# A conv mixer on one core, without three TensorE products per image whose result nothing reads

## The reference: what is computed

```python
h = _layernorm(x, n1_g, n1_b)
p = h @ w_in + b_in                                   # 96 -> 192 channels
local = conv(p, k_conv, 3x3, SAME, one filter per channel)
mixed = 0.25 * (lr + rl + tb + bt) + local            # four decaying scans over the image
mixed = _layernorm(mixed, on_g, on_b)
x = x + (mixed @ w_out + b_out)                       # 192 -> 96 channels
```

## Time and profile before

| | us |
|---|---|
| median of 3 runs | 1312.41 |
| lowest and highest | 1305.92, 1313.32 |
| profiled execution | 1309.46 |
| its span | 1307.7 |
| mixer, first transpose to the last residual | 247.5 to 405.8 |

### The profile page before, as it was taken

The page is one execution under the profiler, slowest core; times in us unless marked ns, Lnnn a source line. Parts: engine busy times, 40 slices in busy tenths (PEclk is TensorE's granted clock), DMA queues, the critical chain, the costliest instruction groups (busy, mean ns, idle before and its releaser), DMA issues. The chain is left out here.

```text
span 1307.7 us, 23695 instructions
## 1 busy us (share of the span) xinstructions
PE 1154.8 (88%) x8859; PEld 790.6 (60%) x8859; DVE 740.0 (57%) x2112; ACT 515.9 (39%) x839; POOL 387.1 (30%) x584
## 2 busy tenths in 40 slices
PE   4888879789887979999999997788888978999998
PEld 2565656566665656766666674466455544577776
DVE  3788844477772436666666666276455565333322
ACT  1555533343431333333343332345343422455543
POOL 3645445443425421010101210424100000353522
PEclk8999969899997989999999998699799999999999
DMA  4500000000000000000000000000000000000000
GB/s 88 100 11 2 2 2 0 1 1 1 2 1 1 0 1 1 1 1 1 1 1 1 1 2 1 1 1 1 1 2 1 2 2 1 2 13 7 9 11 13
DMA packets 28924, 9.39 MB, mean 7 GB/s; under 512 B 26961, under 2 KB 28816, under 8 KB 28816
## 3 DMA queue, kind: packets, MB, share of 16 engines
q1 hardware_dynamic: 25760, 7.02, 2.6%
q10 hardware_dynamic: 3056, 0.92, 0.3%
HBM read 6.36 MB, written 1.57 MB: 6 GB/s over the span
## 5 line engine op out<-in xcount | busy, mean ns | idle before, releaser
L156 POOL TENSOR_TENSOR ln_v<-MV,eps 128x2 f32<-128x2 f32 (+3 forms) x81 | 16.2, 201 | 427.2 <-PE bank L1132 247.3
L1194 ACT ACTIVATE fa_e<-bank 128x1024 f32<-128x1024 f32 x64 | 65.5, 1024 | 161.1 <-PE bank L1102 161.1
L1997 PEld LDWEIGHTS bank<-e_w,ex_G 128*128 128x128 f32 x768 | 90.6, 192 | 14.4 <-issue 14.1
L2112 DVE SCALAR_TENSOR_TENSOR X<-bank,ex_L,X 128x96 f32<-128x96 f32 x128 | 31.8, 311 | 114.0 <-PE bank L1997 108.1
L1246 DVE TENSOR_REDUCE fa_z<-bank 128x4 f32<-128x1024 f32 x64 | 78.3, 1223 | 26.3 <-PE bank L1084 24.7
L1989 PE MATMUL bank<-hT,e_w 96*128 96x512 f32 x192 | 90.6, 609 | 0.0
L1997 PE MATMUL bank<-e_w,ex_G 128*128 128x96 f32 x768 | 90.0, 274 | 0.0
L2040 ACT ACTIVATE ex_G<-bank,e_b 128x512 f32<-128x512 f32 x96 | 64.3, 686 | 61.7 <-PE bank L1989 58.9
L1844 DVE TENSOR_REDUCE ca_z<-bank 128x2 f32<-128x256 f32 x96 | 48.9, 552 | 49.3 <-PE bank L1571 49.2
L1102 PE MATMUL bank<-fa_a,fa_b 64*128 64x256 f32 x512 | 74.1, 409 | 1.1 <-DVE fa_a L1253 1.1
L1115 PE MATMUL bank<-fa_e,fa_v 128*64 128x256 f32 x512 | 72.0, 404 | 1.1 <-ACT fa_e L1194 1.1
(11 more groups left out here) (252 smaller groups left out, 2641.7 us busy)
## 6 DMA issues: line engine op xcount, KB each, us to landing
out_tokens<-X SPq DMA_DIRECT2D x8, 192.0 KB, 2.1
X<-in_x SPq DMA_DIRECT2D x56, 24.0 KB
e_w<-in_L_ffn_w SPq DMA_DIRECT2D x2, 576.0 KB
bias0r<-in_L_conv_rpb_table ACTq DMA_DIRECT2D x16, 24.0 KB
m0w<-in_L_conv_mlp_w SPq DMA_DIRECT2D x2, 144.0 KB
m1w<-in_L_conv_w SPq DMA_DIRECT2D x2, 144.0 KB
f_w<-in_L_ffn_W SPq DMA_DIRECT2D x2, 142.5 KB
mixer<-in_mixer SPq DMA_DIRECT2D x1, 256.0 KB
```

What stands on the lines that cost most here:

```text
L1194: act.activation(E[v % 2][:], k.banks[:, b:b + 2, :].rearrange("p i (c q) -> p i c q", c=2), ACT.Exp).then_inc(s["exp"], 1)
L1997: last = pe.matmul(bank[4 + e % 2][:, t * C:(t + 1) * C], G[e % 2][:, j, t * P:(t + 1) * P], k.ew2[:, e, j, :], start=(j == 0), stop=(j == ...
```

## The change

Three calls of `keep_warm` are deleted. Nothing else is different: every wait, every other product, every buffer and their order stay, on all engines. The loop has 18 steps, and `back` and `conv_t` are each called 16 times, so 50 instructions go.

```diff
                 def back(n):
-                    keep_warm(pe, k, bank[4][:])
                     pe.wait_ge(s["z2"], n + 1)
                     after(pe, s["zTe"], n)
...
                 def conv_t(n, slot):

-                    keep_warm(pe, k, bank[4][:])
                     pe.wait_ge(s["conv"], 9 * (n + 1))
                     pe.wait_ge(s["acc1"], n + 1)
...
                 for n in range(IMAGES + 2):
                     slot = n % 2
-                    keep_warm(pe, k, bank[4][:])
                     if n + 1 < IMAGES:
                         tokens(n + 1, 1 - slot)
```

## The result

The median of 12 runs is 1316.15 us, against 1310.71 us for 12 runs of the kernel before. The medians are 5.4 us apart. The ratio on record is 1.0053, with a 95% interval of 1.0029 to 1.0078; it is that of the means, which are 7 us apart. The change made the kernel slower by 5 to 7 us of 1311, which is within 1% and clear of no change. The profiled execution took 1312.8 us, with a span of 1311.0 us where the one of before had 1307.7.

The account below looks back on a forecast made before the run. TensorE was the busiest mixer engine, with its path and ScalarE's `cm_zT` ending level before `out`. From 1309.5 us, minus 0.3 gain, plus 12.8 for clock falls, gave 1322.0; a third of 2.95 made it 1323, range 1307 to 1336.

Parts of the forecast that it names:

- The product ahead of the wait for `cm_z` costs nothing: Mixer, unread product before TensorE waits for VectorE's norm: removing it gains 0, as the wait ends at the same time.
- The other two gain nothing because `cm_zT` ends level with TensorE's path: Products ahead of `conv_t` and `tokens`: TensorE's path shortens 0.43 us an image, but ScalarE's copy limits gain to 0.3 us together.
- The rival of a gain of 6 us: Mixer: clock holds and `out` starts 0.43 us earlier in each image, giving 1303.5 us; chance 0.04.
- The price of a cold stretch: Taken from window attention: each stretch at low clock costs 1.60 us, with two stretches counted to a fall in the mixer.
- the 10.5 or more that were named as a sign: Between two mixer residuals, an image with a cold stretch was to take 10.5 us or more, against 8.97 to 8.99.
- Eight cold stretches: Mixer: idle gaps make the clock fall in one image in four, 4 falls of two stretches, 12.8 us of loss.
- the 4 to 8 stretches that were to support it: Mixer's granted clock: 4 to 8 stretches at 0.50, beginning near the transposes of `cm_z`, were to support the forecast.
- A fall in nearly each image: Rival for the mixer: longer gaps around the transposes make the clock fall almost every image, 24 us, 1333 us; chance 0.21.
- what was said of them there: A skill page on PE-mode transposes: they do not count as engine activity as products do, giving more falls weight; no size.
- The clock holds: Rival for the mixer: the waits are too short for the clock to fall, 1309 us, no change; chance 0.20.
- The third of 2.95 us that was added for the median of before: Whole kernel: the median of runs lay 2.95 us above the profiled execution; a third of this was added, giving 1323 us.

Follow-up runs that it names:

- the gate was opened: Against the changed kernel: one residual product of `out` ahead of its wait for `cm_zT`, which is signalled in halves, old order kept; 1304.33 us.
- the open form: Against the changed kernel: `out`'s residual products ahead of its wait, `cm_zT` signalled in halves, sums in two PSUM banks, no unread products; 1292.62 us, ratio 0.9877.
- The second profile: The kernel without the unread products executed once more under the profiler, nothing else changed; 1311.59 us.
- the kernel with both sums in one bank: Against the changed kernel: `out`'s residual products ahead of its wait, `cm_zT` signalled in halves, both sums opened in one PSUM bank; 1291.89 us, ratio 0.9881.

## Why the prediction was right, and where it was off

The forecast was 1323 us, with a range of 1307 to 1336. The measured 1316.15 lies in it and is slower than before, within 1%. The mechanism was right, an unchanged path and a few falls of the clock, and the term for the falls was more than twice too large; it is a wide range that covers it.

- *The product ahead of the wait for `cm_z` costs nothing.* Right: the idle time there went from 0.92 to 1.14 or 1.15 us, as predicted. The kernel with three products in this gap shows the same from the other side.
- *The other two gain nothing because `cm_zT` ends level with TensorE's path.* Right: images stayed at 8.98 to 8.99 us, `out` waits 0.32 us in each, and the gain came out once the gate was opened (8.40 us) and went when the products were put back into the open form (8.07 to 8.50). The rival of a gain of 6 us fell for the reason that was given against it.
- *The price of a cold stretch, 1.60 us, two to a fall.* Two to a fall was right. The price was a little high: the first fall made two images 2.7 us longer together, 1.3 us a stretch, and they took 10.2 and 10.4 us by their residuals, not the 10.5 or more that were named as a sign.
- *Eight cold stretches.* This term was mis-sized. It rested on four falls, one image in four, and the profile has two falls, of two stretches each, which is the lower end of the 4 to 8 stretches that were to support it. Two falls at 2.7 us are 5.3 us in place of 12.8. With the 1 us that was added for the median this gives 1309.5 - 0.3 + 5.3 + 1 = 1315.5 us, and the median was 1316.15. That the two come within 1 us is partly luck, since single runs differ by several us. The second profile had three falls, not all of them long. Even for window attention the rate was high: the two windows in the earlier trace rows are 48 us apart, one fall in five images. Taking the rate over from a stage with longer waits, 1.43 us, to one with shorter, 1.14 and 0.32, had no row behind it.
- *A fall in nearly each image* did not come. The kernel with the new order of `out` behind its full wait, which idled 1.47 us ahead of one of its falls, came nearest to it with four falls in the mixer. No run isolates a stretch of transposes, so what was said of them there stays untested.
- *The clock holds* was the rule of the page TensorE: Matmul & The Clock Gate of the Trainium skill, section "HAM oscillation — how this bites in real kernels". The falls in the steady part of the mixer followed waits shorter than those it names (1.14, 0.32 and, once, 1.47 us), so it does not hold here either.
- *The third of 2.95 us that was added for the median of before* was about right. With 12 runs that median is 1310.71, 1.25 us above the profiled execution.

What stays open: which image falls. Two executions fell first at the same image, ten alike before it did not, and the shorter image of 8.07 us with the same 1.14 us of waiting did not fall in the steady part at all.

## What to carry to other kernels

An unread product on TensorE has two prices. On the path it costs the distance to the next start (0.22 us here, not the 0.38 us of its row), and only if nothing else releases the next step at the same time; in front of a wait it costs nothing. So before such products are taken out as waste, look whether the clock ever falls elsewhere in the kernel behind a wait of the same size; and if they are worth keeping, put them ahead of a wait that TensorE has in any case, and look at the clock up to the end of the stage. The larger gain lay beside them: the row of the step that started level with two releasers (`out`) pointed to a gate worth 0.58 us an image, more than the products.

## What the runs showed of the hardware

The order of products with different weights changed how long they take. When its data is there, `out` with weights of 128, 128 and 64 rows in turn holds TensorE for 1.91 us (324.65 to 326.56 in the kernel with the gate alone opened). With the residual's two products first and then the two of each kind together it is 1.57 us (323.45 to 325.02 in the kernel with both sums in one bank). Behind the full wait the two orders take 2.01 us (338.55 to 340.56 after the change) and 1.67 us (314.03 to 315.70 with the order alone), 0.34 apart again. No run here tells what the 0.34 us are; that the loads of weights are the cause is only an assumption.

In the steady mixer a fall of the clock followed idle times of 1.14 and 0.32 us with light work between them, although TensorE was busy for 0.84 of the stage by the profile. The share of busy time alone did not tell: the kernel with 8.07 us an image was busy 0.83 and held its clock.
